# Last attention in another order of inverse sums and output rows, and half of the context keys computed behind the barrier of the expert phase

## What is computed

```python
# layers 1 to 3 attend to the context: keys and values of the context, 3 layers, each batch
k = (key @ Wk.T).reshape(Bq, Nk, HEADS, HEAD_DIM).transpose(0, 2, 1, 3)
v = (value @ Wv.T).reshape(Bq, Nk, HEADS, HEAD_DIM).transpose(0, 2, 1, 3)
...
# layer 0, feed-forward: each token goes to its best 2 of 8 experts
mid = jax.nn.gelu(flat @ exp_W1[e] + exp_b1[e], approximate=False)
y_e = mid @ exp_W2[e] + exp_b2[e]
...
# layer 3, the last attention: 4 heads chosen per batch, 64 channels each, 1024 x 1024 scores
scores = jnp.einsum('bksd,bktd->bkst', Qk, Kk) / jnp.sqrt(jnp.float32(dh))
attn = jax.nn.softmax(scores, axis=-1)
out = jnp.einsum('bkst,bktd->bksd', attn, Vk)
out = out.transpose(0, 2, 1, 3).reshape(B, S, K * dh)
return out @ Wo + bo
```

## Time and profile before

| what | value |
|---|---|
| median of 3 runs (lowest, highest) | 4048.69 us (4042.71, 4053.03) |
| the profiled execution, its own time | 4052.79 us |
| its span from first to last instruction | 4051.0 us |
| PE, share of the span in which it is busy | 85% |
| DVE | 57% |
| ACT | 38% |
| POOL | 11% |
| mean granted clock of PE | 0.933 of 2.4 GHz |

### The profile page before, as it was taken

One profiled execution on the slowest core, in us unless ns is written; L12 is line 12 of the kernel. 1 busy time (PEld: TensorE's weight loads), 2 busy tenths in 40 slices (PEclk: granted clock), 3 DMA queues, 4 the chain that ended last, 5 costly groups with the idle time before them and its releaser, 6 DMA issues.

```text
span 4051.0 us, 55117 instructions
## 1 busy us (share of the span) xinstructions
PE 3435.7 (85%) x21294; PEld 1848.5 (46%) x21294; DVE 2300.9 (57%) x5198; ACT 1527.5 (38%) x2358; POOL 426.6 (11%) x323
## 2 busy tenths in 40 slices
PE   7788788888788489998898878898888988879988
PEld 5333433433433378886455324453244533344532
DVE  7664664674674456665634566534657246663356
ACT  5353344334334234443543224423334332254322
POOL 0000001001001234442000120000300002100002
PEclk9899999889889799999999989999999989999989
DMA  7401400410420587775011311113021032201130
GB/s 277 114 10 54 128 10 21 154 17 8 149 36 21 152 209 230 221 223 139 11 27 29 68 27 38 27 27 69 2 54 37 1 43 54 53 11 27 27 69 11
DMA packets 197241, 292.19 MB, mean 72 GB/s; under 512 B 88124, under 2 KB 154318, under 8 KB 180240
## 3 DMA queue, kind: packets, MB, share of 16 engines
q1 hardware_dynamic: 179957, 268.10, 25.2%
q0 software_dynamic: 17024, 20.53, 2.5%
HBM read 210.02 MB, written 77.23 MB: 71 GB/s over the span
## 4 chain that ended last, share of the span: by engine, by line
PE 55%; DVE 24%; ACT 8%; DMA 7%; issue 4%; SPq 1%; POOL 1%; another core or an unknown queue 0%; DVEq 0%; ACTq 0%; POOLq 0%
PE ps L877 6%; DVE max_parts L2101 5%; PE ps L827 5%; PE ps L829 5%; PE ps L828 5%; PE ps L1036 4%; PE ps L1265 3%; PE ps L1272 3%; PE ps L996 3%; PE ps L1158 2%; PE ps L1419 2%; DMA q_stack<-in_exp_W 2%; PE ps L1019 2%; PE ps L1193 2%; ACT arena L1538 2%
## 5 line engine op out<-in xcount | busy, mean ns | idle before, releaser
L877 PE MATMUL ps<-ternary_W,ident 128*128 128x512 f16 x2260 | 679.1, 416 | 134.9 <-ACT arena L1665 41.4
L2101 DVE TENSOR_REDUCE max_parts<-ps 128x1 f32<-128x512 f32 (+3 forms) x768 | 383.3, 550 | 156.3 <-PE ps L999 114.9
L1538 ACT ACTIVATE arena<-ps 128x256 f32<-128x256 f32 (+7 forms) x512 | 318.5, 650 | 405.1 <-PE ps L1019 234.6
L877 PEld LDWEIGHTS ps<-ternary_W,ident 128*128 128x128 f16 x2260 | 227.5, 105 | 454.7 <-issue 152.0
L1852 POOL TENSOR_TENSOR arena<-arena 128x640 f32<-128x640 f32 x96 | 154.8, 1613 | 1993.4 <-ACT arena L1770 1992.3
L2021 DVE CAST arena<-arena 128x256 f16<-128x256 f32 (+2 forms) x424 | 160.8, 379 | 259.7 <-ACT arena L1702 139.3
L1604 ACT ACTIVATE arena<-ps 77x1024 f32<-77x1024 f32 x192 | 190.4, 1016 | 197.0 <-PE ps L1185 194.2
L1770 ACT ACTIVATE arena<-ps 128x1024 f32<-128x1024 f32 x128 | 130.5, 1023 | 333.7 <-PE ps L1408 332.0
L2023 DVE TENSOR_TENSOR arena<-arena 128x256 f16<-128x256 f32 (+2 forms) x424 | 242.6, 572 | 14.7
L2536 DVE TENSOR_REDUCE max_parts<-ps 128x1 f32<-128x512 f32 x256 | 166.2, 686 | 143.5 <-PE ps L1392 141.7
L1702 ACT ACTIVATE arena<-ps,arena 128x256 f32<-128x256 f32 x312 | 147.8, 474 | 260.5 <-PE ps L829 239.4
(11 more groups left out here) (444 smaller groups left out, 7394.9 us busy)
## 6 DMA issues: line engine op xcount, KB each, us to landing
arena<-scr_expert_weights SPq DMA_DIRECT2D x52, 1024.0 KB
k_stack<-scr_expert_weights SPq DMA_DIRECT2D x26, 1024.0 KB
q_stack<-in_exp_W SPq DMA_DIRECT2D x16, 1024.0 KB
scr_expert_weights<-k_stack SPq DMA_DIRECT2D x16, 1024.0 KB, 4.9
q_stack<-scr_q SPq DMA_DIRECT2D x108, 128.0 KB, 3.9
scr_q<-arena SPq DMA_DIRECT2D x48, 256.0 KB, 2.3
k_stack<-scr_q SPq DMA_DIRECT2D x72, 128.0 KB, 4.8
scr_q<-arena SPq DMA_DIRECT2D x16, 512.0 KB, 4.3
```

Source lines behind the costliest of these rows:

```text
L877: pe.matmul(s[:, 0:CH], ident[:], Wq1[:, 0, 0:CH], start=True, stop=True)
L1538: act.activation(PR[:, n % NP, kt * P:T], slot(L, "ST", g, kt, j)[:, kt * P:T], ACT.Exp).then_inc(*did("act", L, "exp", g, kt, j))
L2101: dve.tensor_reduce(mpart[:, j * NT + t, c:c + 1], slot(L, "S", g, t, j, c)[:, 0:n], AX, ALU.max).then_inc(*frees("dve", L, "S", g, t, j, c))
```

## The change

In the last attention `ON h-1` moves from kt 3 of head h to kt 6 (heads 1 and 2) or kt 2 (head 3). For heads 0 to 2 the sum `PA` also takes in the last block of keys, kt 7, one more addition on DVE and one on POOL, and `SB` then multiplies one piece instead of two. The output rows of a head are computed in one step `W h`, in which PE alternates between the lower and the upper 64 rows; the bias products follow for two blocks at a time.

The context keys of batches 2 and 3 (`LATE`) are computed at the start of phase 1 on PE, ACT and DVE, ahead of the experts. SP stores them between the table and the weights of tile 2. The mask is computed ahead of the keys' split on DVE instead of behind it. Two buffers of the values move (`vxs`), and ACT no longer waits for DVE before it reuses a buffer of keys.

```diff
-            if h and kt == 3:
+            if h and kt == (6 if h + 1 < HS else 2):
                 steps += [("ON", h - 1)]
         steps += [("PV", h, NT - 1)]
-    return steps + [("SB", HS - 1), ("WS", 0), ("WS", 1), ("WS", 2), ("ON", HS - 1), ("WB", 0), ("WB", 1), ("WB", 2), ("WL",)]
+        if h + 1 < HS:
+            steps += [("PA", h, NT - 1)]
+    return steps + [("SB", HS - 1), ("W", 0), ("W", 1), ("W", 2), ("ON", HS - 1), ("W", 3)]
+
+
+def last_sum(h):
+
+    return NT - 1 if h + 1 < HS else NT - 2
...
-            for i in range(3):
+            for i in range(2):
                 tile_table(i)
                 tile_weights(i)
+            tile_table(2)
+            for n in LATE:
+                store_context_keys(n)
+            tile_weights(2)
+            sp.wait_ge(*of("st_kx", LATE[-1], 1))
+            sp.wait_ge(*of("st_vx", LATE[-1]))
...
+            def head_output(h):
+
+                if h == 0:
+                    for p, name in enumerate(("S0", "S1", "B0", "B1")):
+                        banks[p] = claim(name, "F3", "W", p)
+                pe.wait_ge(*of("dve", "F3", "onlo", h))
+                for t in range(TCH):
+                    outs = [banks[(c * TCH + t) // 2][:, t % 2 * D:(t % 2 + 1) * D] for c in range(2)]
+                    for n, (a, b_) in enumerate(((0, 0), (0, 1), (1, 0))):
+                        for c in range(2):
+                            r = slice(DS * c, DS * (c + 1))
+                            mm = pe.matmul(outs[c], ON4[r, a, h, t * P:(t + 1) * P], Wp[r, pi["F3o"], b_, h, :], start=h + n + t % 2 == 0,
+                                           stop=h + 1 == HS and n == 2, skip_group_check=True, tile_position=(DS * c, 0))
...
-            context_keys()
+            context_keys(EARLY)
             batch_end(pe, "pe")

             fresh()
             led.phase, led.batch = 1, 0
+            context_keys(LATE)
             experts()
...
-                        for n, p in enumerate((PA4[h % 2], PR4[:, (h * NT + NT - 1) % NP])):
+                        parts_of_sum = [PA4[h % 2]] + [PR4[:, (h * NT + kt) % NP] for kt in range(last_sum(h) + 1, NT)]
+                        for n, p in enumerate(parts_of_sum):
...
-                    for kt in range(1, NT - 1):
+                    for kt in range(1, last_sum(h) + 1):
```

More of the change, by code:

```diff
@@ L17 @@
 NG, GH = 4, 4
+EARLY, LATE = (0, 1), (2, 3)
 TX = 104
@@ L1107, in difference_attention, with context_keys @@
                     mm.then_inc(*did("pe", "A", "W", t))
-            def context_keys():
-                pe.wait_ge(*of("ld_kvw", "context", NB - 1))
-                pe.wait_ge(*of("dve", "cts"))
-                for n in range(NB):
+            def context_keys(batches):
+                if batches == EARLY:
+                    pe.wait_ge(*of("ld_kvw", "context", NB - 1))
+                    pe.wait_ge(*of("dve", "cts"))
+                for n in batches:
                     for l, L in enumerate(XL):
@@ L1561, in own_attention, with context_keys @@
                 exps(L, own_attention_steps(led.batch > 0))
-            def context_keys():
-                act.wait_ge(*of("ld_kvw", "context", NB - 1))
-                act.activation(cts[:, 0], ct4, ACT.Copy).then_inc(*did("act", "cts_hi"))
-                for n in range(NB):
+            def context_keys(batches):
+                if batches == EARLY:
+                    act.wait_ge(*of("ld_kvw", "context", NB - 1))
+                    act.activation(cts[:, 0], ct4, ACT.Copy).then_inc(*did("act", "cts_hi"))
+                for n in batches:
                     for l, L in enumerate(XL):
@@ L2177, in tile_tables, with context_keys @@
                 dve.wait_ge(*of("dve", "tiles"))
[L2179 to L2184 removed]
+            def context_keys(batches):
+                if batches == EARLY:
+                    dve.wait_ge(*of("act", "cts_hi"))
+                    dve.tensor_tensor(cts[:, 1], ct4, cts[:, 0], ALU.subtract).then_inc(*step("cts"))
+                    tile_tables()
+                    dve.wait_ge(*of("ld_kvw", "context", NB - 1))
+                    dve.tensor_scalar(maskb, maskr.unsqueeze(2).broadcast_to([1, NB, NH, TC]), 0.0, -BIG, ALU.is_gt, ALU.mult).then_inc(*step("mask"))
+                for n in batches:
                     dve.wait_ge(*of("act", "free", "KX", n, len(XL) - 1, KD - 1))
```

69 lines of the change are left out of this document (24 added, 45 removed).

## The result

The changed kernel takes 4012.22 us in the median of six runs (3996.26 to 4022.49), the kernel before in the same comparison 4046.51 (six runs, 4038.45 to 4058.57): ratio 0.9914, 95% interval 0.9889 to 0.994, so 24 to 45 us or 0.9% faster. I forecast 3986 and the range 3970 to 4010: the direction is right, but the measured gain is little more than half of the forecast one (34 us by the medians for 63). The profiled execution took 4007.55 us, its span is 4005.7 at a mean clock of 0.934, against 4051.0 before at 0.933.

What follows compares the result with a forecast made beforehand. PE was taken to bound the kernel, directly or waiting for DVE. Terms gave -12.8 us per batch, -51.2 for four, and -11.9 at the barrier: -63.1 from 4052.8, then 4.1 lower for the median, 3986; range 3970 to 4010.

Steps and rivals of the forecast that it cites:

- (a): Heads 1 and 2 of the last attention: PE's two kt 4 waits go with their clock loss, -13.9 us per batch.
- (c): Start of head 2: new PE wait behind `pad_keys` and `ON 0` on DVE, clock loss included, +8.4 us per batch.
- (d): From `MT 3` to `SB 3`: later `SB 2` costs nothing, earlier `ON 2` removes the wait before `SB 3`, -1.2 us per batch.
- (e): Output rows: the two halves overlap in pairs, first residual at +7.3 instead of +11.5 us, -4.2 us per batch.
- (b): `SB` of heads 0 to 2 multiplies one piece, added `PA` hidden; -1.9 us per batch for `SB 0` and `SB 1`.
- (f): Boundary of phases 0 and 1: half the context keys move behind the barrier, which opens earlier, -11.9 us in all.
- R1: Rival at the output rows: the two halves do not overlap, +17 us, 4003 us; chance 8%.
- R4: Rival in head 2: the clock stays low after the new wait, +82 us, 4068 us, slower than before; chance 4%.
- R3: Rival at head 2's start: the new wait is longer because `ON` is contended, +15 us, 4001 us; chance 10%.
- R5: Rival in the heads: another unseen PE wait replaces the removed ones, +34 us, 4020 us, or some 4040; chance 5%.
- R2: Rival in phase 1: moved keys not hidden, or SP's late queue holds up a tile, 11.9 us lost, 3998; chance 14%.

Runs made afterwards that it cites:

- `ON` at 6 alone: The kernel before with only the inverse sums of heads 0 and 1 moved to key tile 6 of the next head: 4017.8 us, ratio 0.9943.
- two-piece sum: The changed kernel without the added eighth partial addition, so every `SB` multiplies two pieces: 4001.2 us, ratio 0.9897.
- either part alone: Two kernels, the kernel before with only the last attention's hunks (4005.9 us, ratio 0.9909) or only the moved context keys (4040.6 us, ratio 0.9996).

## Why the forecast of 3986 was too low

**The place was right, the sum was not.** M allows a ledger per batch, from runs that differ in one of its rows each (and in the moved keys, which lie outside M):

| step | forecast | measured | from |
|---|---|---|---|
| (a) and (c) | -5.5 | -5.7 | `ON` at 6 alone, less before |
| (d), (e): `ON 2` earlier, rows in pairs | -5.4 | -4.5 | two-piece sum, less `ON` at 6 alone |
| (b): eighth addition, one-piece `SB` | -1.9 | +1.4 | changed, less two-piece sum |
| sum | -12.8 | -8.7 | |

PE's idle time in M tells the same without the work: 15.3 us before, 11.6 with `ON` at 6 alone, 11.7 with the two-piece sum, and 15.2 again in the changed kernel. What (a) and (c) won in waiting, (b) gave back. What is left is busy time: three `SB` shorter by 0.95 us, and the rows in pairs (104.1 us busy, 108.1 when not paired), 6.9 us together; the other 1.8 of the 8.7 are not taken apart.

**(a)** right: both waits of 4.54 us went. Their clock loss went with them, but the new waits brought their own, and the mean granted clock over M is 0.96 before and after.

**(c)** right as a mechanism and, in the kernel where it stands alone, in size: 5.46 us of wait. In the changed kernel it is 7.37 us in place of the 6.4 foretold, because `pad_keys` took 4.74 us and not 3.7. I took the 3.7 from a row in which an addition of POOL ran beside the first of the four instructions (2346.07 to 2347.61, that one took 1.56 us, the other three 0.78 each), and did not ask what a second such addition would do. The clock loss was 2.6 us in batch 4 and 2.2 in the mean (I had 2.4).

**(b)** is the step that failed, by 3.3 us per batch and 13 us in all. It put the added `PA` "beside `PV` and the wait for the maxima's rows" and so at nothing. On DVE that addition stands behind `pad_keys` and `ON`, in the very queue that (c) had found to be late, and on POOL it runs beside `pad_keys` and stretches it. That makes 1.36 us for the stretched `pad_keys` and 0.66 for one more `PA`, the 2.0 us between the waits of 7.37 and 5.35. I had priced the added addition by the time of PE and not by that of the engine which I had just shown to bound the place. And its price while POOL adds was misread: 3.77 us for four are one of 1.79 beside POOL and three of 0.56, not four of 0.94.

**(d)** for `SB 2` I had 0.8 to 1.2 us of delay paid back by a shorter `SB`. It waited 1.97 us. The row names no releaser, but `PA 2 7` on DVE ended 0.1 us ahead of it, at 3974.49, and had taken 1.70 us beside an addition of POOL of 1.68; at the 0.56 that it takes alone the wait would have been 0.8. The earlier `ON 2` brought 0.75 us of the 1.2: 0.45 us of wait are left ahead of `SB 3`, where three of DVE's five `PA` took 1.7 to 1.8 us each and not 0.94. From `MT 3` to `SB 3` PE took 22.4 us with the two-piece sum, but 23.3 to 24.4 in the changed kernel, more than the 22.9 of before (23.4 in one batch).

**(e)** right: a step of 0.98 us as computed, 7.47 us to the residual for 7.3, and 4.0 us less than before for 4.2, of which the pairing is 3.1 (10.56 to 7.47); I had put the rest at about nothing. The rule of the Trainium skill (TensorEngine Tiling, Key Properties), that a change of tile does not drain TensorE, agrees with the paired rows: six alternating products in 0.50 us.

**(f)** was over-sized: -11.9 forecast, -6 by the mean of five ratios, -5 on top of the attention's part, and none in the first comparison, where M alone gives 35 us for the 34 measured. The barrier did open earlier, and PE went from the late keys straight to tile 0 at once, both as foretold. "I cost both at nothing" was said of SyncE's late queue and the transfers behind it; the wait it led to was 7 to 13 us at tile 3, visible in the profile, and yet cutting it by more than half returned nothing that could be measured. That the expert phase takes back a part of the early start is shown; which of its steps does is not settled.

Of the rivals, R1 and R4 are refuted: the halves overlap, and the clock recovers in 6.4 us. R3 did not come as drawn, since `ON` took its short 5.4 us; the contention hit `pad_keys` instead. R5's wait in kt 4 did not come; the one ahead of `SB 2` did, as counted under (d). R2 came in part, a held-up tile included. Together, (b) with 13 us and (f) with 6 to 12 make up most of the 29 us between the forecast gain and the measured one; (e) and (d) add 3 to 4. The range failed since its upper end covered one rival and not two errors of the same sign. The 2 us by which 4012 lies beyond it are less than the scatter (the same kernel measured again gave 4008), the 26 us from the forecast are not.

## What to carry to other kernels

Once an engine is found to be late at a place, price every operation that the change adds to its queue there at its full length, and look at what its neighbour engine does at the same time. If two long pieces of work stand end to end on the engine that others wait for, move one of them a stage earlier: here 7.4 us of wait became 2.0 and 2.7. For a change of tens of microseconds in a kernel that scatters by ten, find a stretch between two marks that repeats to some tenths and keep a ledger in it, idle time and busy time apart; variants that differ by less than the scatter belong in one group of runs.

## What the runs showed of the hardware

- The same four half-precision multiplications of DVE (128 x 616 each) took 3.38 and 3.39 us with POOL adding beside only the first 0.6 us, 3.69 where it did so for 0.9 us, and 4.74 with a second addition of POOL's (128 x 640, 1.92 us) inside them. An addition of 128 x 384 took 0.56 us alone and 1.70 beside one of POOL's of 1.68 us, ending 0.42 us after it.
- After waits of 4.54 us and more PE resumed with products of 0.61 us (all but one of eight before, all four each in the changed kernel, with `ON` at 6 and with two pieces), and the granted clock over the next 6.4 us was 0.51 to 0.77. After waits of 2.0 to 2.7 us it was 0.51, 0.73 or 1.00, and where it was 0.73 the first product still took 0.39 us. So waits of these lengths cost between nothing and 3 us beyond themselves.
- Two issues of context-key stores on SyncE took 0.96 us in one place (1372.77, before, transfers' share 0.35 from 1370 to 1376) and 4.12 in another (1390.46, after, share 1.05 while they were issued).
- Outside the marks of M, a batch of phase 2 took 406 to 418 us in eight profiles (before, changed twice, either part alone, rows not paired, two-piece sum, `ON` at 6 alone), 410 to 418 in those of before and after. The scatter of 10 us between executions lies mostly there and in phase 1, not in the last attention.
